# A two-layer transformer kernel in fp32 on one core: where VectorE, ScalarE and GpSimd prepare the last feed-forward, and in which order TensorE enters it

## The reference

```python
h = layernorm(x) * (1 + ca) + sa
x = x + ga * L1_attn(h)            # linear attention: (Q @ KV) * Z, then @ Wo.T + bo
h = layernorm(x) * (1 + cb) + sb
# feed-forward, INTER = 1408 = 11 chunks of 128
g = (h @ gate_w.T) * gate_s
u = (h @ up_w.T) * up_s
out = ((silu(g) * u) @ down_w.T) * down_s
x = x + gb * out
```

## Time and profile before

| | us |
|---|---|
| median of 3 runs | 1993.18 |
| lowest and highest | 1989.17, 1996.96 |
| profiled execution, its own time | 1995.52 |
| its span, first to last instruction | 1993.7 |
| PE busy in the span | 1905.1 |
| output projection and feed-forward of layer 1, from the first matmul of `zb_step` to the end of the span | 447.3 |

### The profile page before, as it was taken

How to read it: one execution, slowest core, us unless ns; L and a number is a source line. 1 busy time by engine, 2 the same in 40 slices (tenths; PEclk the granted TensorE clock), 3 DMA queues, 4 the chain that set the end, 5 groups by cost and what they waited for, 6 DMA issues and landing times. The chain is left out here.

```text
span 1993.7 us, 26372 instructions
## 1 busy us (share of the span) xinstructions
PE 1905.1 (96%) x9936; PEld 1367.3 (69%) x9936; DVE 1163.8 (58%) x1948; ACT 707.2 (35%) x1275; POOL 775.3 (39%) x730
## 2 busy tenths in 40 slices
PE   7999999999999999899999999998998878998998
PEld 5677555544555545788888888887886667776887
DVE  5466877666666733854434443445333767777776
ACT  4221355545555564521111111114221244343332
POOL 1122778788776589200000000002001556664662
PEclk9999999999999999999999999999999989999999
DMA  9852422322321203200001010002000011111211
GB/s 326 267 150 107 97 54 55 86 55 55 86 45 33 60 19 99 69 33 32 32 1 32 32 32 1 1 19 74 6 6 11 22 32 53 54 48 43 95 54 48
DMA packets 80783, 120.83 MB, mean 61 GB/s; under 512 B 7008, under 2 KB 38768, under 8 KB 80624
## 3 DMA queue, kind: packets, MB, share of 16 engines
q1 hardware_dynamic: 73200, 93.96, 16.5%
q0 software_dynamic: 7456, 25.18, 4.2%
HBM read 93.68 MB, written 25.44 MB: 60 GB/s over the span
## 5 line engine op out<-in xcount | busy, mean ns | idle before, releaser
L1795 DVE TENSOR_REDUCE part_max<-banks 128x1 f32<-128x512 f32 (+2 forms) x640 | 357.0, 614 | 149.3 <-PE banks L1767 91.0
L2320 ACT ACTIVATE probs<-banks 128x512 f32<-128x512 f32 (+3 forms) x640 | 311.0, 539 | 269.0 <-PE banks L2235 133.4
L1767 PE MATMUL banks<-kst,qst 96*128 96x512 f32 (+2 forms) x640 | 261.4, 417 | 12.1 <-DVE part_max L1795 9.7
L2231 PE MATMUL banks<-qst,kst 98*128 98x512 f32 (+2 forms) x640 | 251.4, 413 | 0.7 <-ACT probs L2320 0.6
L1429 POOL TENSOR_TENSOR w_lo<-early_weights,w_hi 128x512 fp32r<-128x512 f32 x4 | 5.1, 1302 | 544.1 <-ACT w_hi L1403 544.1
L763 DVE TENSOR_TENSOR tokens_b<-banks,tokens_b 128x512 f32<-128x512 f32 x64 | 44.3, 691 | 251.6 <-ACT tokens_b L678 251.6
L2181 POOL TENSOR_TENSOR early_weights<-probs 128x512 f32<-128x512 f32 (+2 forms) x152 | 160.6, 1089 | 56.4 <-ACT probs L2320 56.0
L2181 POOL TENSOR_TENSOR pairs_own<-probs 128x512 f32<-128x512 f32 (+2 forms) x152 | 157.3, 1068 | 63.4 <-ACT probs L2320 63.2
L678 ACT ACTIVATE tokens_b<-banks 128x512 f32<-128x512 f32 x64 | 38.2, 597 | 395.7 <-PE banks L229 395.7
L2231 PEld LDWEIGHTS banks<-qst,kst 98*128 98x128 f32 x640 | 123.6, 194 | 64.3 <-issue 49.0
L1767 PEld LDWEIGHTS banks<-kst,qst 96*128 96x128 f32 x640 | 123.5, 193 | 59.9 <-DVE part_max L1795 46.7
(11 more groups left out here) (251 smaller groups left out, 4211.9 us busy)
## 6 DMA issues: line engine op xcount, KB each, us to landing
tokens_a<-in_L_wmod SPq DMA_DIRECT2D x12, 1024.0 KB, 7.1
qst<-q_hi SPq DMA_DIRECT2D x32, 256.0 KB, 5.7
kst<-k_hi SPq DMA_DIRECT2D x32, 256.0 KB, 8.3
tokens_b<-in_down_wt SPq DMA_DIRECT2D x10, 512.0 KB, 3.7
q_hi<-qk_out_hi POOLq DMA_DIRECT2D x16, 256.0 KB, 3.4
q_lo<-qk_out_lo POOLq DMA_DIRECT2D x16, 256.0 KB, 3.4
k_hi<-qk_out_hi POOLq DMA_DIRECT2D x16, 256.0 KB, 4.1
k_lo<-qk_out_lo POOLq DMA_DIRECT2D x16, 256.0 KB, 4.3
```

The lines of the kernel that those rows point to most:

```text
L1767: mm = nc.tensor.matmul(dst[:, 0:wide], qst[n % QS][0:BIASROW, h, P * t:P * t + P], kst[(NB * g + c) % KS][0:BIASROW, h, 0:wide], start=Tr ...
L1795: nc.vector.tensor_reduce(part_max[:, n % 2, ht, c:c + 1], max_bank(slot)[:, 0:wide], AX_X, ALU.max).then_inc(max_read, 1)
L2231: mm = nc.tensor.matmul(dst[:, c0:512], kst[ck % KS][0:BIASROW + 2, h, at:at + P], qst[n % QS][0:BIASROW + 2, h, c0:512], start=True, stop ...
L2320: nc.scalar.activation(probs[:, q % PS, h, c0:512], score_bank(sh)[:, c0:512], ACT.Exp, scale=SCALE).then_inc(exp_done, 1)
```

## The change

Layer 1 alone is touched.

- **First rest.** `out_p.lo_vector(0)` comes ahead of the rests of weight blocks 1 to 3; GpSimd begins its bias sums only behind that rest (`parts_ready`), and a `zb_step` waits only for its own block's `spread`.
- **Transposes.** Those of block 2 leave the place behind the output products and come in halves behind products 0 and 1 of unit 0; those of block 3 come in halves behind products 0 and 3 of unit 1. The `z_vector` of block 3 moves into unit 0 of the feed-forward, its `rows_scalar` into unit 1.
- **Entry on VectorE.** The low halves of unit 0's weights and the four token sums of pass 0 move from GpSimd to VectorE, spread over blocks 1 and 3; `scales_vector` moves to block 1. ScalarE casts unit 0's weights in block 1 ahead of `rows_scalar(0)` instead of in block 2. In each block `std_scalar(b - 1)` now stands behind `hi_scalar(2 b + 2)`. Token operands of pass 0 go in the order 0, 1, 6, 3, 2, 4, 5.
- **Raw weights of unit 1** get memory of their own and are loaded as soon as all output products are done.
- **Segments.** They begin at chunks 0, 2, 4, 5, 7, 9: the one-chunk segment is the third of a pass, not the last. Segment 0's down weights are cast in unit 1 instead of 0. In the last unit the tiles are placed 1, 1, 2.
- **Second pass.** Its token operands are no longer made in one batch in unit 10 and two in unit 11; they are spread one by one over units 10 and 11.

```diff
             SEGS = (NCH + 1) // 2
+            SEG_AT = [0, 2, 4] + list(range(5, NCH + 1, 2))
-            FIRST_ORDER = (0, 1, 6, 3, 4, 2, 5)
+            FIRST_ORDER = (0, 1, 6, 3, 2, 4, 5)
...
                 def sync(sp):
+                    sp.wait_ge(out_p.multiplied, T)
+                    Stage.load_unit(sp, 1)
                     sp.wait_ge(b_ready, 7)
-                    Stage.load_unit(sp, 1)
+                    sp.wait_ge(t_step, 4)
                     Stage.load_down(sp, 0)
...
                 def gpsimd(pool):
                     Stage.weight_sums_gpsimd(pool, 0)
-                    for i in range(4):
-                        Stage.weight_lo_gpsimd(pool, 0, i)
-                    for i in range(4):
-                        Stage.token_sum_gpsimd(pool, 0, i)
...
+                def first_weight_lo_vector(dve):
+                    for i, (lo, hi) in enumerate(BATCH):
+                        dve.wait_ge(a_hi_s, i + 1)
+                        nc.vector.tensor_tensor(a_lo[:, lo:hi, :, :], raw(0, lo, hi), a_hi[:, lo:hi, :, :],
+                                                ALU.subtract).then_inc(a_ready, 1)
...
                         for j in range(4):
                             gate_up(u, j)
-                        if u == 0:
-                            last_norm()
+                            if u == 0 and j < 2:
+                                turn(NB - 2, j)
+                            if u == 1 and j in (0, 3):
+                                turn(NB - 1, j // 3)
...
                     for u in range(UNITS):
                         if u:
                             silu(u - 1, 1)
-                        snapshot(u)
-                        if u:
+                            Stage.snapshot_scalar(act, u)
                             hidden_hi(u - 1, 1)
                             Stage.weight_hi_scalar(act, u, 3)
...
                         silu(u, 0)
-                        if u == 0:
+                        if u == 1:
                             last_h()
...
                         q, c = segment(u)
-                        if c == 0:
+                        if c == (q == 0):
                             down_hi(q)
...
                         add_trunk2(u)
+                        add_gate1_part(u)
+                        if u == 0:
+                            last_z()
...
-                        if u == NCH - 1:
-                            for j in range(4):
-                                Stage.operand_lo_vector(dve, 1, j)
...
-                    if b:
+                    if 0 < b < NB - 1:
                         norm.tensor(pe, b - 1)
...
             def scalar(act):
                 out_p.hi_scalar(act, 1)
                 for b in range(NB):
+                    if b + 1 < NB:
+                        out_p.hi_scalar(act, 2 * b + 2)
                     if b:
                         norm.std_scalar(act, b - 1)
                     if b + 1 < NB:
-                        out_p.hi_scalar(act, 2 * b + 2)
                         out_p.hi_scalar(act, 2 * b + 3)
                     if b == 1:
+                        for i in range(4):
+                            ffn.weight_hi_scalar(act, 0, i)
                         rows_scalar(act, 0)
...
+                    if b == NB - 1:
+                        ffn.token_sum_vector(dve, 0)
+                        ffn.operand_lo_vector(dve, 0, 6)
+                        ffn.token_sum_vector(dve, 1)
+                        ffn.operand_lo_vector(dve, 0, 3)
                     if b:
                         statistics(dve, b - 1)
...
                         for i in range(G):
                             attend(dve, i)
+                        out_p.lo_vector(dve, 0)
                         out_p.merged_vector(dve, range(1, KT))
-                        out_p.lo_vector(dve, 0)
```

139 lines of the change are left out of this document (81 added, 58 removed).

## The result

| | before | after |
|---|---|---|
| median, us (runs) | 1996.09 (10) | 1981.26 (10) |
| lowest and highest | 1989.17, 2003.87 | 1980.53, 1988.87 |
| profiled execution, its own time | 1995.52 | 1980.84 |
| its span | 1993.7 | 1978.6 |

The ratio is 0.9938, with a 95% interval of 0.9923 to 0.9954: the change takes 0.6%, 12 us, off the time. The medians differ by 14.8 us and the profiled executions by 14.7 us. The sum had 22.3. The direction is right and the time lies inside the range (1961 to 1982), though only just: a third of the gain is missing by the traces, and nearly half by the ratio.

What follows compares the result with a forecast made beforehand. TensorE, busy 1905.1 of 1993.7 us, was taken as the bound, so only its losses could be won back. 0 - 11.2 - 7.5 - 3.6 = -22.3 gave 1973.2 from 1995.5, forecast 1971 as median, range 1961 to 1982.

Steps and rivals of the forecast that it cites:

- Part 1, first rest: Output projection: first product starts 2.1 us earlier, gain gone by product 5; worth 0, between -2 and +3 us.
- Part 2, entry: Output products 6 and 7 to unit 2: transposes moved, token sums on VectorE; -11.2 us, bounds gain 2.6 to 15.9.
- rival of long entry chains: Entry: VectorE's eight extra instructions at 2.30 us or ScalarE's rows late; part 2 gains only 2.6, 1979.5 us; chance 0.15.
- slower rival: Between 1578 and 1650 short waits keep TensorE's clock at 1.2 GHz, 0.20 us more per matmul; up to 2009 us; chance 0.04.
- Part 3, second pass and segments: Units 10 to 12 and the moved short units: -7.5 us in sum, bounds -12 and +2.
- Units 16 and 17, "I charge 1.0 us": Short pair: chain reaches add_up0 at 16.3 us, product 3 wants its bank at 16.4; loss charged 1.0 us.
- Units 5 to 7, "as much as units 5 to 7 lose now": Unit 5 loses about 2 us by the split beside a token sum, units 6 and 7 another 1: 3.0 as before.
- Units 10 to 12, "4.5": Waits for spread token rests in unit 11 add to 3.8 us, 4.5 with the clock, against 8.4 + 4.6 before: -8.5.
- the short units lose as before: Rival: units 5, 6, 16 and 17 lose 4.6 us a pair, pass change 6.8; gain 13, 1980 us; chance 0.13.
- the lower bound of -12: Part 3's best case: nothing lost in the second pass and short units, -12 us.
- From the sum to the median: The runs' median was taken as 2.3 us below the profiled execution, so 1973.2 became 1971 us.
- Part 4, tail: Last unit: tiles of 6 matmuls fill the banks while the first add_x is awaited, clock stays up; gain 3.6, bounds 2 and 4.

Runs made afterwards that it cites:

- e10_balanced: Changed kernel with two of the eight down tiles in units 4 and 15 moved to units 5 and 16: median 1981.30 us, ratio 0.9936.
- e6_sums_3_8: Changed kernel with GpSimd's four token sums of pass 1 in units 3 and 8, two each, instead of 3 to 6: 1983.13 us, ratio 0.9944.
- e1_odd_last: Changed kernel with the one-chunk segment back at the end of each pass and the last unit's tiles as before: 1979.74 us, ratio 0.9935.
- e15_small_rests: Changed kernel with pass 1's token rests made on only 16 of 512 columns, most of that splitting left out: one execution, 1975.83 us.
- e7_first_rest_only: Kernel before with only context rest 0 ahead of the weights' rests, bias sums behind it, zb_step waiting for its own spread: 1993.78 us, ratio 1.0000.
- e11_combined: Changed kernel with std_scalar ahead of casts, pass 1 token sums in units 3 and 8, tiles spread around one-chunk segments, pass 1's segment first: 1975.57 us, ratio 0.9897.
- e14_weights_gpsimd: Changed kernel with unit 0's weights cast in block 2 again and their low halves back on GpSimd: 1982.87 us, ratio 0.9931.

## Why the prediction was right in two parts and wrong in the third

**Part 1, first rest: right.** Forecast 2.1 us at the first output product and nothing at product 5. Measured 2.0 and 0.8 us in the changed kernel, -0.1 to 0.8 in the eight kernels with its entry; alone, 2.5 and -0.3, with a ratio of 1.0000.

**Part 2, entry: right in sum, by two misses that cancel, and right in most of its waits.** Forecast -11.2 to unit 2, measured -10.7. But unit 0 begins 2.6 us earlier than worked out (66.0 where 1615.1 is 68.7 from the first `zb_step` before), since product 6 begins 1.0 us earlier than worked out, and products 6 and 7 take 11.0 us where 12.5 was counted; and units 0 and 1 take 34.7 us where 31.6 was worked out. Token sums on VectorE take mostly 1.22 us, the price that I took. Unit 0 begins behind product 7 without a wait. Operand 5 costs 2.32 us (2.2 forecast), the first low half of unit 1 on GpSimd 1.58 (no wait forecast), the rows in unit 1 3.99 (3.1). The rival of long entry chains falls. What the prediction did not name is which wait this replaces: the root behind casts behind GpSimd's queue. It followed the new order and never the old one, so it could not say that with either of two moves taken back most of the gain would stay.

**The clock: right.** The lower level lasts some five matmuls behind the wait of 3.99 us, and the granted clock is 0.97 from the first `zb_step` to product 6 and 0.96 from there to unit 2, where the same stretches had 0.94 and 0.88 before. The slower rival falls.

**Part 3, second pass and segments: the step that failed**, +0.5 instead of -7.5. It failed in three terms.

- *Units 16 and 17, "I charge 1.0 us".* They cost 3.2. The chain was followed from the last product to `add_up0` and product 3's bank, 16.3 against 16.4, and that was right: no wait stands there. It was not followed on: hidden, `add_gate1` for product 4's bank (0.81), the weight cast behind it, and GpSimd's last low half for product 5 (1.14) and for the next unit (0.60). The loop takes 18.4 + 11.2 us without a wait for TensorE, and `e10_balanced` shows what the length of the units does here: with 12 matmuls more in the first of them the same chain costs 0.6.
- *Units 5 to 7, "as much as units 5 to 7 lose now".* They lose 5.5 us, where 3.0 was forecast (0.5 more lies in units 2 to 4). The 2 us for the split beside the token sum were right (2.24), and `e6_sums_3_8` removes them alone. On top come the same short-pair waits, 0.47, 1.12 and 0.63, for which the sum had 1 us in units 6 and 7. The two causes do not simply add up: `e1_odd_last`, with the sums and without short units there, loses 4.5 us in units 5 to 7.
- *Units 10 to 12, "4.5".* They lose 8.0. (The loss before was 13.7 and not 8.4 + 4.6: the windows of the earlier trace rows hold three matmuls of neighbouring units, 92 and 109 for 90 and 108. So 0.7 of the 3.5 is in the old loss, and 2.8 is missing from the gain.) The waits for the rests are the ones named, 2.37, 0.38, 1.42 and 0.65, 4.8 us against 3.8; the rests of products 2, 3 and 4 are ready 5.4, 8.6 and 13.1 us after unit 11 begins, where 3.1, 6.5 and 10.5 were worked out. Behind the first wait six matmuls run at the lower level, some 1.3 us; behind the others the clock stays up (granted 1.00 from 1796.40 to 1810.10) and only the first matmul or two start late. VectorE enters unit 10 some 5.5 us behind TensorE, with unit 9's split and adds, and has no slack to make it up; `e15_small_rests` gives 5.6 of the 8.0 back. That the late start alone explains the difference to 4.5 was not tried.

So the rival "the short units lose as before" (4.6 a pair, pass change 6.8, 1980 us) came nearest: 3.3 and 5.5 a pair, pass change 8.0, 1981.26 us. Its own sum is off, though: 2 x 4.6 + 6.8 is 16.0, as much as 3.0 + 8.4 + 4.6 before, so its terms give part 3 as 0 and not as +2; measured +0.5. Nor is the lower bound of -12 "nothing lost", which would be -16.

**From the sum to the median: off by 2.7 us.** I took the median as 2.3 us below the profiled execution, from three runs. With ten runs of the kernel before it is 0.6 above that execution (1996.09), and in the changed kernel 0.4 above (1981.26 against 1980.84). With the 7.6 us missing from the sum this is the distance from 1971.

**Part 4, tail: right.** -3.6 forecast and measured. Of this, 1.9 us are the wait and 1.6 the lower clock behind it, and the second part is in some traces only: in `e7_first_rest_only` the same wait of 1.91 us is followed by no such matmul. `e1_odd_last` undoes the move and gets the time back in the short units' place: 3.6 us in the tail against 1.8 in units 2 to 9 and 3.3 in units 13 to 17, and the total is nothing that the ratios can tell.

**Open.** What the 2.4 us are that units 10 to 12 lose even with small rests, and why the loop enters unit 5 late in `e11_combined`, was not tried.

## What to carry to other kernels

A loop that runs without waits does so at one length. Where some iterations get shorter, follow the chain that closes the loop through every engine and on to the last operand of the next iteration, not to the first bank only, and count it over a whole period: here it takes some 29 us for two units, which two of 15.0 us hold and two of 12.3 do not. Evening the lengths out took 2.7 of 3.3 us away at one pair (e10) and left 3.9 us at another, which the loop entered late (e11); moving the short segment only carried the loss elsewhere. Where work is added at a stage border, read from the timeline when each engine really enters the stage. And a tiny instruction that sits in a queue behind work for someone else, like the 0.20 us square root, can come 6 us late and hold a stage's start: look at what stands ahead of it, since cutting the chain at one place may do.

## What the runs showed of the hardware

How long a subtraction takes beside GpSimd, and who pays, varies more than I had expected. On VectorE the hidden multiply takes 0.75 or 2.12 us, the pair of down splits 1.95 or 3.89, a token rest 1.22 or 1.81. In other places GpSimd pays: in `e14_weights_gpsimd` the four low halves, which took 6.00 us before, take 9.14 beside VectorE's sums and rests, whose times do not change (timeline of GpSimd, then of VectorE):

```profile
1604.80 9.14 POOL L1017 TENSOR_TENSOR w_a_lo<-early_weights,w_a_hi 128x512 fp32r<-128x512 f32 x4 [25.84 <-ACT w_a_hi L1012]
```

```profile
1605.06 1.21 DVE L1044 TENSOR_TENSOR w_b_lo<-tokens_b,w_b_hi 128x1024 fp32r<-128x1024 f32 x1
1606.19 1.21 DVE L970 TENSOR_TENSOR w_t<-tokens_b,w_t 128x1024 f32<-128x1024 f32 x1
```

An add that reads one input from an accumulator bank is not slowed by GpSimd's low halves (POOL L1015, from 1787.49 for 3.42 us); the multiply behind it, with both inputs in SBUF, is (timeline of VectorE in the changed kernel):

```profile
1788.53 0.68 DVE L1191 TENSOR_TENSOR w_sums<-banks,w_sums 128x512 f32<-128x512 f32 x1
1789.30 1.02 DVE L1205 SCALAR_TENSOR_TENSOR w_act<-w_sums,w_us 128x512 f32<-128x512 f32 x1
```

The Trainium skill (SBUF — State Buffer, "Who interferes with whom") says that a VectorE instruction with two SBUF inputs contends with a GpSimd instruction that reads SBUF, and one with at most one SBUF input does not, outside the faster two-port modes. The traces agree: 2.12, 3.89 and 1.81 us on the one side, 0.68 on the other. The same section says that the order of issue decides who is blocked; no run here was made to show that.

The clock is no fixed price of a wait either: behind a wait of 1.91 us nine matmuls ran at the lower level in the kernel before and none in `e7_first_rest_only`.
